# Three of eight product sums moved to GpSimd, the low parts to VectorE, and another order of the work

## What is computed

```python
x = x + _L0_conv_ref(_gn(x), ...)   # adaptive 3x3 filter
x = x + _L1_conv_ref(_gn(x), w1, w2, w3)   # three 3x3 convolutions, 32 -> 64 -> 64 -> 32

# first layer, for each pixel l, R = 4 filters r, S = 9 taps s
mu = softmax(gate)                                  # from x, a 1x1 product
kern = exp(-(pu / sig_u) ** 2 - (ps / sig_s) ** 2)  # from x: angle and widths per pixel and filter
w = mu * kern / (sum(mu * kern) + 1e-06)
v = value_w @ x
agg = einsum('brsl,bcsl->brcl', w, patches(v))
out = pw_w @ agg + pw_b
```

## Time and profile before

| | |
|---|---|
| median of three runs | 565.48 us (565.24 to 566.05) |
| the profiled execution | 566.55 us, of which the span of its instructions is 564.7 us |
| VectorE busy | 461.2 us, 82% of the span |
| TensorE busy | 479.0 us, 85% |
| ScalarE, GpSimd busy | 220.7 us, 79.5 us |
| mean granted clock of TensorE | 0.949 |

### The profile page before, as it was taken

How to read it: one execution, slowest core, us unless ns; L and a number is a source line. 1 busy time by engine, 2 the same in 40 slices (tenths; PEclk the granted TensorE clock), 3 DMA queues, 4 the chain that set the end, 5 groups by cost and what they waited for, 6 DMA issues and landing times.

```text
span 564.7 us, 6912 instructions
## 1 busy us (share of the span) xinstructions
PE 479.0 (85%) x2440; PEld 381.1 (67%) x2440; DVE 461.2 (82%) x571; ACT 220.7 (39%) x419; POOL 79.5 (14%) x72
## 2 busy tenths in 40 slices
PE   2503545379999999999999999999999999998995
PEld 1302423258788878887878787878787887786894
DVE  2379999999999999999999999999999999510000
ACT  2331331327442653265416632573257304331320
POOL 1401230223021302130213021302040100000000
PEclk9999855589999999999999999999999999999999
DMA  4100001241123411431144114412441044025202
GB/s 141 41 1 0 4 1 37 58 97 41 39 48 91 80 51 39 102 76 49 41 96 87 30 50 100 87 25 56 100 91 24 16 107 88 22 68 116 46 0 38
DMA packets 40274, 32.22 MB, mean 57 GB/s; under 512 B 26160, under 2 KB 30768, under 8 KB 40240
## 3 DMA queue, kind: packets, MB, share of 16 engines
q1 hardware_dynamic: 40240, 31.78, 24.2%
HBM read 5.66 MB, written 4.19 MB: 17 GB/s over the span
## 4 chain that ended last, share of the span: by engine, by line
DVE 43%; issue 23%; PE 21%; SPq 4%; DMA 3%; ACT 3%; POOL 1%; POOLq 0%; DVEq 0%
DVE prod L663 14%; PE conv_ps L331 14%; DVE prod L672 14%; SPq L252 3%; DMA xraw<-in_x 3%; DVE st L506 2%; DVE x L682 2%; PE geo_ps L351 1%; PE agg_ps L390 1%; PE geo_ps L357 1%; SPq L222 1%; PE val_ps L375 1%; POOL vs L938 1%; PE conv_ps L343 1%; DVE trig L610 1%
## 5 line engine op out<-in xcount | busy, mean ns | idle before, releaser
L663 DVE TENSOR_TENSOR prod<-val_ps,tapw 128x2048 f32<-128x2048 f32 x80 | 181.0, 2279 | 1.2 <-PE val_ps L375 0.9
L331 PE MATMUL conv_ps<-c_hi,wc_hi 128*128 128x448 f32 (+2 forms) x384 | 152.3, 397 | 0.0
L672 DVE TENSOR_TENSOR prod<-prod 128x2048 f32<-128x2048 f32 x64 | 146.4, 2287 | 0.4
L331 PE MATMUL conv_ps<-c_lo,wc_hi 128*128 128x448 f32 (+2 forms) x384 | 144.1, 375 | 0.0
L331 PE MATMUL conv_ps<-c_hi,wc_lo 128*128 128x448 f32 (+2 forms) x384 | 144.1, 375 | 0.0
L938 POOL TENSOR_TENSOR vs<-vn 128x1024 f32<-128x1024 f32 x32 | 69.5, 2182 | 146.9 <-PE val_ps L375 138.5
L331 PEld LDWEIGHTS conv_ps<-c_hi,wc_hi 128*128 128x128 f32 x384 | 72.5, 189 | 18.0 <-ACT c_lo L867 5.4
L331 PEld LDWEIGHTS conv_ps<-c_hi,wc_lo 128*128 128x128 f32 x384 | 72.2, 188 | 10.7
L331 PEld LDWEIGHTS conv_ps<-c_lo,wc_hi 128*128 128x128 f32 x384 | 72.5, 189 | 10.2 <-issue 1.2
L867 ACT ACTIVATE c_lo<-conv_ps 128x512 fp32r<-128x512 f32 (+4 forms) x88 | 41.9, 486 | 74.4 <-PE conv_ps L343 74.1
L375 PE MATMUL val_ps<-ident_sb,vs 128*128 128x128 f32 x256 | 44.3, 302 | 24.2 <-DVE prod L663 24.2
(11 more groups left out here) (105 smaller groups left out, 477.6 us busy)
## 6 DMA issues: line engine op xcount, KB each, us to landing
xq_hi<-y_hi SPq DMA_DIRECT2D x128, 66.0 KB, 2.0
xq_lo<-y_lo SPq DMA_DIRECT2D x128, 66.0 KB, 2.1
xraw<-in_x SPq DMA_DIRECT2D x32, 128.0 KB, 2.7
x2r<-x SPq DMA_DIRECT2D x128, 32.0 KB, 1.9
out_y<-x2r SPq DMA_DIRECT2D x32, 128.0 KB, 2.8
prod<-in_w SPq DMA_DIRECT2D x1, 576.0 KB, 5.2
vn<-vn SPq DMA_DIRECT2D x16, 24.8 KB, 1.8
prod<-in_w SPq DMA_DIRECT2D x1, 384.0 KB, 3.3
```

Source lines behind the costliest of these rows:

```text
L331: mm = nc.tensor.matmul(bank[:, 0:conv_cols(n)], weights, lo if part == 1 else hi, start=term == part == 0, stop=final and part == 2)
L663: v.tensor_tensor(dst, val.unsqueeze(2).to_broadcast([P, B, R, C]), wgt.unsqueeze(3).to_broadcast([P, B, R, C]), ALU.mult).then_inc(mult_d ...
L672: v.tensor_tensor(product(i, a), product(i, a), product(i, b), ALU.add).then_inc(add_done, 1)
```

## The change

There are five parts.

1. `SUMS` says who adds each product: GpSimd (G), VectorE (V), or nobody (T), in which case `transpose_sums` transposes several products into the same place of the bank, which adds them. In image 0 one add of each half is on GpSimd and three are T; in the seven other images three of eight are on GpSimd, five on VectorE. The products have seven buffers in place of six, and `mult` waits for those that it overwrites.
2. The low parts of all nine chunks are `lo = bank - hi` on VectorE. `take_high` and the copy on ScalarE issue nothing any more.
3. `geometry` reads `xc` and stands ahead of `v_product` in `geo_ps`; `v_product` waits for `tap_weights` part 0 to have read it.
4. `trig2` is gone: the squares are written over `trig`.
5. The lists of all engines are in another order.

```diff
-UNIT_TAP = (0, 1, 2, 3, 4)
 ADDS = ((0, 1), (2, 3), (0, 2), (0, 4))
-LEFT = (0,)
-UNIT_BUF = (0, 1, 2, 1, 1)
-N_PROD = 3
+SUMS = [("GTTT", "GTTT")] + [("GGVV", "GVVV")] * (IMAGES - 1)
+UNIT_BUF = (0, 1, 2, 3, 1, 4, 5, 6, 3, 5)
+N_PROD = 7
...
+LOW_V = [tuple(range(N_SPLIT))] * IMAGES
...
+        def wait_added(eng, i, h, n):
+
+            if SUMS[i][h][n] == "V":
+                eng.wait_ge(add_v, adds_by("V", i, h, n + 1))
+            elif SUMS[i][h][n] == "G":
+                eng.wait_ge(add_g, adds_by("G", i, h, n + 1))
+
+        def wait_consumed(eng, i, h, n):
+
+            if SUMS[i][h][n] == "T":
+                eng.wait_ge(agg_t, 8 * i + G * (h + 1))
+            else:
+                wait_added(eng, i, h, n)
+
+        def left(i, h):
+
+            return [0] + [b for (a, b), who in zip(ADDS, SUMS[i][h]) if who == "T"]
...
             def v_product(i, h):
                 if h == 0:
-                    pe.wait_ge(xn_done, i + 1)
+                    pe.wait_ge(ch_v, CH_V * i + 1)
...
-                    for b in LEFT:
+                    for b in left(i, h):
...
             def mult(i, u):
...
+                if u == 8:
+                    wait_consumed(dve, i, 0, 1)
+                if u % TAPS == 4:
+                    wait_consumed(dve, i, h, 0)
...
+            def low_part(j, n):
+                if n not in LOW_V[j]:
+                    return
+                dve.wait_ge(hi_done, N_SPLIT * j + n + 1)
+                for src, hi, lo in split_parts(j, n):
+                    op = v.tensor_tensor(lo, src, hi.bitcast(F32), ALU.subtract)
+                op.then_inc(lo_v, 1)
...
@@ GpSimd @@
+            def add_products(i, h, n):
+                if SUMS[i][h][n] != "G":
+                    return
+                a, b = ADDS[n]
+                pool.wait_ge(mult_done, UNITS * i + TAPS * h + max(a, b) + 1)
+                for m in range(n):
+                    if a in ADDS[m]:
+                        wait_added(pool, i, h, m)
+                p.tensor_tensor(product(i, TAPS * h + a), product(i, TAPS * h + a), product(i, TAPS * h + b),
+                                ALU.add).then_inc(add_g, 1)
```

More of the change, by code:

```diff
@@ L352, in v_product @@
                                  start=True, stop=True).then_inc(v_mm, 1)
[L354 to L359, removed]
             def values(i, u):
-                h, tap = u // TAPS, UNIT_TAP[u % TAPS]
+                h, tap = u // TAPS, u % TAPS
                 if u >= 2 or i >= 1:
@@ new lines, in body @@
+                convs(i - 3, 40, 42)
+                on(i - 1, values, 4)
+                convs(i - 3, 42, 43)
+                on(i - 1, take_high, 6)
+                convs(i - 3, 43, 46)
+                on(i - 1, values, 5)
+                convs(i - 3, 46, 50)
+                on(i, geometry)
+                convs(i - 3, 50, 52)
+                on(i - 1, values, 6)
+                on(i, take_high, 3)
+                on(i, v_product, 0)
+                on(i, take_high, 1)
+                convs(i - 3, 52, 53)
@@ L466, in body @@
[L466 to L479, removed]
@@ L748, in body @@
-                on(i + 1, tap_weights, 3)
+                on(i - 4, gn2_bias)
+                on(i - 2, gn1_scale)
+                on(i - 3, mult, 1)
+                on(i - 3, mult, 2)
+                on(i - 5, low_part, 7)
+                on(i, add_products, 0, 0)
+                on(i - 5, low_part, 8)
+                on(i - 3, mult, 3)
+                on(i - 2, gn1_bias)
+                on(i - 3, add_products, 1, 0)
+                on(i - 4, split_low)
+                on(i - 3, mult, 4)
@@ new lines, in body @@
+                on(i - 4, low_part, 1)
+                on(i - 3, mult, 9)
+                on(i - 4, low_part, 2)
+                on(i - 3, add_products, 1, 1)
+                on(i - 4, low_part, 3)
+                on(i - 3, add_products, 1, 2)
+                on(i - 2, tap_weights, 4)
+                on(i - 3, add_products, 1, 3)
+                on(i - 2, tap_weights, 5)
+                on(i - 3, residual, 0)
+                on(i - 4, low_part, 4)
+                on(i - 2, split_weights)
@@ new lines, in body @@
+                on(i - 3, gn2_stats, 0)
+                on(i + 4, add_products, 0, 1)
+                on(i - 2, tap_weights, 6)
+                on(i - 3, residual, 1)
+                on(i - 4, low_part, 5)
+                on(i - 3, gn2_stats, 1)
+                on(i - 2, tap_weights, 7)
+                on(i - 3, gn2_spread)
+                on(i - 2, mult, 0)
+                on(i - 1, gn1_stats)
+                on(i - 3, gn2_scale)
+                on(i - 4, low_part, 6)
+                on(i - 1, gn1_spread)
@@ new lines, in body @@
+                on(i - 4, sums_out, 5)
+                on(i + 3, low_part, 7)
+                on(i - 3, tap_weights, 5)
+                on(i - 4, sums_out, 6)
+                on(i - 4, sums_out, 7)
+                on(i - 5, high_part, 5)
+                on(i - 5, high_part, 6)
+                on(i - 4, norm2)
+                on(i - 4, split_high)
+                on(i - 5, high_part, 7)
+                on(i - 5, high_part, 8)
+                on(i - 2, norm1)
+                on(i - 1, low_part, 8)
@@ L910, in _ @@
+                on(i - 2, tap_weights, 0)
+                on(i - 2, v_evict, 0)
+                on(i - 2, tap_weights, 1)
+                on(i - 2, tap_weights, 2)
+                on(i - 2, v_evict, 1)
+                on(i - 3, sums_out, 0)
+                on(i - 14, low_part, 1)
+                on(i - 3, sums_out, 1)
+                on(i - 12, low_part, 5)
             s.preload_act_table_set(EXP_SET)
```

280 lines of the change are left out of this document (133 added, 147 removed).

## The result

The changed kernel takes 572.32 us, the median of four runs (572.01 to 573.15), beside 565.76 for the kernel before on the same chip (four runs, 565.24 to 566.14). The ratio is 1.0129, with a 95% interval of 1.0111 to 1.0148: slower by 1.3%, where 541 was forecast. The profiled execution had 572.6 us, of which the span is 570.8.

The account below looks back on a forecast made before the run. VectorE and TensorE both full in middle images, VectorE alone in image 0, TensorE at the end; gains 2.5 + 7.7 + 3.4 + 5.2 + 4.7 + 2.0 = 25.5 give 541 (forecast's own range 536 to 546, wider 533 to 556).

Parts of the forecast that it names:

- the lock: Port shared by VectorE and GpSimd: VectorE wins at `split_low`, GpSimd waits 1.1 unfelt, third add meets nothing; put at nothing.
- the lock falls the other way: Rival: GpSimd's add 1 takes the port first, `split_low` waits 4.0 in seven images, 28 in all; 569, chance 0.07.
- start: Before image 0: `tap_weights` starts 6.5 us sooner, less new waits; first multiply net 2.5 us sooner, from 0 to 4.
- image 0: Window of image 0: eight adds leave VectorE, 17.6 us, against waits of 9.9; shrinks by 7.7.
- image 1: Window of image 1: three adds less, low parts 0 to 5 and 1.4 of waits more; gain of 3.4.
- image 6, image 7 and the end: Image 6 gains 1.05; earlier `y_hi` transfers make 4.7 less by image 7's `residual`; last convolutions 2.0 less.
- Images 2 to 6: Middle windows: 6.6 off VectorE, 5.1 on, 0.45 of new wait; 56.5 each, a gain of 1.05 each, 5.2 in five.
- GpSimd's add: Price of a GpSimd add of 2048 columns, in SBUF: 4.0 taken; with the skill's 4497 ns the sum stays the same.
- The clock: Rival: TensorE's clock stays low in image 0, 7.5 more for each half of the transposes; 556, chance 0.10.
- old pace: Rival: TensorE, or it and VectorE in turn, keep the pace in middle images; 547, or 550 with dearer low parts; chance 0.18.

Follow-up runs that it names:

- part 3 early: Changed kernel with `tap_weights` part 3 moved ahead of `result` 0 and `mult` 6; 542.99 us when timed again, ratio 0.9603 to the kernel before.
- GpSimd waiting: Changed kernel, VectorE's order kept, GpSimd's add of the second half waiting for `tap_weights` part 3; 542.75 us, ratio 0.9593 to the kernel before.
- the fill unlocked: On part 3 early, two GpSimd pair sums in image 0 wait for VectorE's tap-weights chain; 540.80 us, ratio 0.9569 to the kernel before.

## Why the prediction was wrong, point by point

**The step that failed** is in the part on the lock: "The third add lies beside `mult` 7. I put the lock at nothing." It does not lie beside `mult` 7. `mult` 6 releases it, and `tap_weights` part 3 stands between. I walked the order along `split_low` only, though the price was stated right there: an operation behind the releasing multiply with two operands in SBUF. The runs with part 3 early and with GpSimd waiting put 29 to 30 us on this one place, where the forecast had nothing: 4.4 us in each of seven images. The rival "the lock falls the other way" had the mechanism, 28 us and 569, but at the wrong operation. That its 569 lies near 572.3 is luck as to the place: it charged 4.0 an image to `split_low`, which lost nothing.

**Its argument for safety holds at one place only.** It read in the earlier trace rows that the operation behind a multiply and a tiny one starts 0.04 after the multiply's end, and said that "GpSimd needs a semaphore first". At `split_low` that came true: 0.05 for VectorE, 0.08 for GpSimd. But the margin is 0.03 us, and it hangs on the length of the operation between. Behind L566, of one column, the second operation starts 0.12 after it and wins; behind L640, of 128 columns, it starts 0.20 after it and loses. Of the rule cited from the Trainium skill ("SBUF — State Buffer", Who interferes with whom), an exclusive lock with issue order deciding, the trace agrees at every place looked at.

**The other terms** can be read in the kernel with part 3 early (us of its profile, beside that of before, cut at the statistics of images 1, 2, 3 and 7):

| | before | part 3 early | gained | forecast |
|---|---|---|---|---|
| start | 41.54 | 39.91 | 1.6 | 2.5 |
| image 0 | 55.75 | 46.80 | 9.0 | 7.7 |
| image 1 | 57.40 | 57.17 | 0.2 | 3.4 |
| images 2 to 5 | 229.92 | 225.14 | 4.8 | 4.2 |
| image 6, image 7 and the end | 180.09 | 172.08 | 8.0 | 7.8 |
| sum | 564.70 | 541.10 | 23.6 | 25.5 |

Transposes of the sums in image 0 of the changed kernel:

```profile
59.84 5.40 PE L427 MATMUL agg_ps<-ident_sb,prod 128*128 128x128 f32 x48
...
74.08 8.22 PE L427 MATMUL agg_ps<-ident_sb,prod 128*128 128x128 f32 x64
```

- *Start*: near. The forecast had counted "one or two waits of up to 2.0", and two came, 1.8 each at L644 and L645, from the same lock. The first multiply of the changed kernel starts at 37.13 (near 37 was forecast). With the fill unlocked the statistics of image 1 are at 37.44, 4.1 sooner than before.
- *Image 0*: better than forecast by 1.3. In the changed kernel 48 transposes took 5.40, and 64 took 8.22, so 0.11 to 0.13 each where 0.12 was taken; the waits at `mult` 8 and `residual` 1 with part 3 early were 2.1 and 2.05, where 2.5 and 3.5 stood.
- *Image 1*: missed. The forecast replaced the 1.8 us in which VectorE had been idle by 1.4 of waits; it was idle 2.5 (0.72 and 0.56 of it at the first norm), and L640 took 1.98 there in place of 0.28, beside a pair sum. These two make 2.8 of the 3.2 that were missed.
- *Images 2 to 6*: the period of 56.5 was right, with 0.35 of wait at `gn1_scale` (0.45 forecast) and TensorE busy 54.9 (55.5).
- *GpSimd's add*: 4.5 to 4.6, above the 4.0 taken and the bound of 4.32. The Trainium skill's 4497 ns for it ("GPSIMD Engine Reference", Performance versus the Vector engine) was the better number; the trace agrees. "The sum stays the same" by it was true of the adds' own path, but the same figure is also the length of the lock.
- *The clock* and the *old pace* did not decide. In image 0 of the changed kernel the granted clock averaged 0.74, but TensorE's long runs of transposes took 0.11 to 0.13 us each, and not the 0.23 of the low level. With part 3 early it averaged 0.99 there. In middle images TensorE kept its high clock once VectorE wasn't held (1.00, against 0.97 in the changed kernel, where TensorE waited 3.1 for `result` 1 behind L641).

## What to carry to other kernels

Where GpSimd gets work on data in SBUF, as its adds did here, its price isn't only its own time but that of every VectorE operation with two SBUF operands that can come while it runs (and of some with one, as L575 in the earlier trace rows): list for each GpSimd instruction what releases it, how long it and what is queued behind it run, and every VectorE operation in that stretch, small ones first. A small operation pays the whole rest of the GpSimd instruction (4.4 us for one of 0.28). Put such operations ahead of the releasing one, or let GpSimd wait for them where it has time; and after any edit, however small, read the durations of the small operations again: three edits here only moved the lock elsewhere.

## What was not expected of the hardware

- GpSimd's instruction released by a multiply and VectorE's second operation behind that multiply start 0.03 us apart, and in each of the middle images of the trace it falls the same way: L757 at 281.70 against 281.73, GpSimd at 298.24 against L641 at 298.27. The four runs lie close together (572.01 to 573.15), so a race of this kind looks like a fixed cost.
- Two back-to-back operations of 0.28 us each can be parted by a GpSimd instruction: L640 took 0.28 and L641 4.67.
- Operations that read a bank kept their pace beside GpSimd's add (`mult` 2.28, `result` 0.68), as forecast; the pair sums (1.9 alone) and the adds (4.6) cost a neighbour with two SBUF operands their whole remainder.
